# Attention and FFN layer on one core: the PSUM banks of scores and maximum products divided 3 and 3 instead of 4 and 2

## What is computed

```python
B, S, D, H, R = (2, 2048, 256, 16, 64)        # head width 16
qkv = layernorm(x) @ W_qkv + b_qkv            # split into q, k, v; q / 4
dist = clip(key - query, -64, 64) + 64
score = einsum('bhqd,bhkd->bhqk', q, k) + einsum('bhqd,qkd->bhqk', q, rel_emb_k[dist])
attn = softmax(score, axis=-1)
ctx = einsum('bhqk,bhkd->bhqd', attn, v) + einsum('bhqk,qkd->bhqd', attn, rel_emb_v[dist])
x = x + ctx @ W_out + b_out
x = x + ffn_fp4(layernorm(x))
```

## Time and profile before

| what | value |
|---|---|
| median of 3 runs | 2591.05 us (2590.91 to 2592.51) |
| the profiled execution | 2594.04 us, its span 2592.3 us |
| PE busy | 2382.4 us, 92% |
| DVE busy | 1930.2 us, 74% |
| ACT busy | 1361.9 us, 53% |
| POOL busy | 606.9 us, 23% |
| DMA, mean over the span | 81 GB/s |
| PE busy in the 40 slices | 7879999999999999999999999999999993899997 |
| granted clock in the 40 slices, tenths | 9959999999999999999999999999999996999998 |

### The profile page before, as it was taken

How to read it: one execution, slowest core, us unless ns; L and a number is a source line. 1 busy time by engine, 2 the same in 40 slices (tenths; PEclk the granted TensorE clock), 3 DMA queues, 4 the chain that set the end, 5 groups by cost and what they waited for, 6 DMA issues and landing times. The chain is left out here.

```text
span 2592.3 us, 47776 instructions
## 1 busy us (share of the span) xinstructions
PE 2382.4 (92%) x19372; PEld 1179.2 (45%) x19372; DVE 1930.2 (74%) x3509; ACT 1361.9 (53%) x1572; POOL 606.9 (23%) x361
## 2 busy tenths in 40 slices
PE   7879999999999999999999999999999993899997
PEld 3424444444444444444444444444444442566665
DVE  6587777777777777777777777777777726899997
ACT  3405555565555555555555555555555561334442
POOL 5402222222222222222222222222222220011111
PEclk9959999999999999999999999999999996999998
DMA  5723323332333333323332332333222221111110
GB/s 159 184 75 86 85 77 85 88 85 76 85 84 96 93 89 101 99 78 85 85 85 82 93 85 77 85 88 85 76 77 77 71 70 54 43 40 49 49 40 27
DMA packets 275656, 210.35 MB, mean 81 GB/s; under 512 B 17058, under 2 KB 266628, under 8 KB 275332
## 3 DMA queue, kind: packets, MB, share of 16 engines
q1 hardware_dynamic: 274308, 203.37, 28.5%
q0 software_dynamic: 1152, 4.19, 0.6%
HBM read 113.35 MB, written 93.34 MB: 80 GB/s over the span
## 5 line engine op out<-in xcount | busy, mean ns | idle before, releaser
L1047 DVE TENSOR_REDUCE amax<-psA 128x1 f32<-128x512 f32 x2048 | 1327.7, 686 | 494.3 <-PE psA L756 485.9
L1017 ACT ACTIVATE probs<-psS 128x1024 f32<-128x1024 f32 x896 | 885.0, 1023 | 483.5 <-PE psS L867 483.0
L756 PE MATMUL psA<-keys,queries 96*128 96x512 bf16 x2048 | 789.0, 392 | 43.8 <-DVE amax L1047 43.6
L867 PE MATMUL psS<-queries,keys 102*128 102x512 bf16 (+7 forms) x2176 | 632.5, 343 | 44.7 <-ACT rel_scores L996 36.8
L780 PE MATMUL psC<-probs,vals 128*32 128x512 f32 (+7 forms) x4352 | 475.0, 524 | 0.6 <-ACT probs L1017 0.6
L756 PEld LDWEIGHTS psA<-keys,queries 96*128 96x128 bf16 x2048 | 196.4, 97 | 500.5 <-DVE amax L1047 439.2
L717 POOL TENSOR_TENSOR band_probs<-band_probs,side 128x2048 f32<-128x2048 f32 x64 | 288.6, 4533 | 559.5 <-PE psC L880 559.5
L867 PEld LDWEIGHTS psS<-queries,keys 102*128 102x128 bf16 (+1 forms) x2176 | 203.4, 99 | 282.0 <-ACT rel_scores L996 98.1
L1012 ACT ACTIVATE band_probs<-psS 128x1024 f32<-128x1024 f32 x128 | 131.1, 1024 | 224.1 <-PE psS L854 224.1
L996 ACT COPY rel_scores<-psS 128x1024 f32<-128x1024 f32 x128 | 129.3, 1012 | 106.9 <-PE psS L769 106.9
L780 PEld LDWEIGHTS psC<-probs,vals 128*32 128x32 f32 (+1 forms) x4352 | 89.1, 102 | 174.0 <-issue 166.5
(11 more groups left out here) (162 smaller groups left out, 2054.2 us busy)
## 6 DMA issues: line engine op xcount, KB each, us to landing
rel_skew<-rel_scores SPq DMA_DIRECT2D x32, 2048.0 KB, 7.5
rel_near<-rel_skew SPq DMA_DIRECT2D x64, 1024.0 KB, 8.1
keys<-k_ring SPq DMA_DIRECT2D x48, 256.0 KB, 5.7
queries<-q_parts SPq DMA_DIRECT2D x192, 64.0 KB, 2.4
ctx_d<-rden SPq DMA_DIRECT2D x32, 256.0 KB, 2.3
ctx_in<-ctx_d SPq DMA_DIRECT2D x32, 256.0 KB, 2.7
q_parts<-parts SPq DMA_DIRECT2D x16, 384.0 KB, 2.9
k_ring<-parts SPq DMA_DIRECT2D x12, 384.0 KB, 3.1
```

The source lines that it names most:

```text
L756: t.matmul(psA[:, n % 2, :], qs[0:NR, qb, h, u * P:(u + 1) * P], keys[0:NR, par, h, c0:c0 + NQ], start=True, stop=True).then_inc(max_ready, 1)
L867: ins = t.matmul(bank[:, o:o + k], keys[0:nr, par, h, c0:c0 + P], qs[0:nr, qb, h, q0:q0 + k], start=True, stop=True, skip_group_check=True)
L1017: ins = a.activation(probs[:, n % 4], src, ACT.Exp)
L1047: v.reduce_max(amax[:, pair, k:k + 1], psA[:, n % 2, :], AX.X).then_inc(max_taken, 1)
```

## The change

`psS` becomes a ring of three banks, each one half of a unit: half number j (numbered on through the whole attention, R units counted as two halves) lies in bank j modulo 3 and waits for half j - 3. The semaphores `unit_ready` and `unit_done` count halves instead of units, so TensorE signals after each half and ScalarE empties each half in an instruction of its own, 512 elements wide; there are twice as many of these. `psA` becomes a ring of three banks, and product n waits for `take` of product n - 3. No arithmetic is changed. SyncE stores each of the three shift rows once its own part is cut: the first after GpSimd's first cast, the second after its second, the third after the last subtract.

```diff
+SBANKS, ABANKS = 3, 3
-        psS = ctx.enter_context(nc.psum_tensor("psS", [P, 4, NQ], F32))
-        psA = ctx.enter_context(nc.psum_tensor("psA", [P, 2, NQ], F32))
+        psS = ctx.enter_context(nc.psum_tensor("psS", [P, SBANKS, NQ], F32))
+        psA = ctx.enter_context(nc.psum_tensor("psA", [P, ABANKS, NQ], F32))
...
-            def store_shift(qb):
-                for r in range(3):
+            def store_shift(m, qb):
+
+                for r, (cut, count) in enumerate(((m_pool, 3 * m + 1), (m_pool, 3 * m + 3), (shift_ready, m + 1))):
+                    wait_alone(sp, passed, cut, count)
                     sp.dma_start(qs[NR + r:NRH:3, qb], shift[:, r, :]).then_inc(shift_in[qb], 16)
...
-                t.matmul(psA[:, n % 2, :], qs[0:NR, qb, h, u * P:(u + 1) * P], keys[0:NR, par, h, c0:c0 + NQ],
+                t.matmul(psA[:, (first + n) % ABANKS, :], qs[0:NR, qb, h, u * P:(u + 1) * P], keys[0:NR, par, h, c0:c0 + NQ],
...
             def rel_products(m, qb, k, at):
 
-                pe.wait_ge(unit_done, at + 1)
                 for i in range(4):
-                    bank = psS[:, 2 * (k % 2) + i // 2, :]
+                    if i % 2 == 0:
+                        pe.wait_ge(unit_done, 2 * at + i // 2 + 1)
+                    bank = psS[:, (2 * at + i // 2) % SBANKS, :]
...
-                def unit_free(n):
-
-                    pe.wait_ge(unit_done, base + place(n, ends) + 1)
+                def half_free(n, half):
+
+                    pe.wait_ge(unit_done, 2 * (base + place(n, ends)) + half + 1)
...
                 def far_half(n, half):
-                    if half == 0:
-                        unit_free(n)
+                    half_free(n, half)
                     step = n // 2
                     h = 2 * (n % 2) + half
-                    bank = psS[:, 2 * (place(n, ends) % 2) + half, :]
+                    bank = psS[:, (2 * (base + place(n, ends)) + half) % SBANKS, :]
...
-                    if half == 1:
-                        ins.then_inc(unit_ready, 1)
+                    ins.then_inc(unit_ready, 1)
...
-                act.wait_ge(unit_ready, at + 1)
-                a.copy(rel[:, 4 * k:4 * k + 4, :].rearrange("p (b x) r -> p b (x r)", b=2),
-                       psS[:, 2 * (k % 2):2 * (k % 2) + 2, :]).then_inc(unit_done, 1)
+                for half in range(2):
+                    act.wait_ge(unit_ready, 2 * at + half + 1)
+                    x = 4 * k + 2 * half
+                    a.copy(rel[:, x:x + 2, :].rearrange("p x r -> p (x r)"), psS[:, (2 * at + half) % SBANKS, :]).then_inc(unit_done, 1)
...
-                v.reduce_max(amax[:, pair, k:k + 1], psA[:, n % 2, :], AX.X).then_inc(max_taken, 1)
+                v.reduce_max(amax[:, pair, k:k + 1], psA[:, (first + n) % ABANKS, :], AX.X).then_inc(max_taken, 1)
```

More of the change, by code:

```diff
@@ L672, in ctx_rows @@
                 return dr.ctx[bass.ds(b * KT + qb * CH, CH), :, gg, :].rearrange("i p t -> p i t")
-            turn_diagonals(0, RUNITS + 2)
-            wait_alone(sp, passed, shift_ready, 1)
-            store_shift(0)
+            turn_diagonals(0, RUNITS)
+            store_shift(0, 0)
             iteration(0, 0)
@@ L764, in rel_products @@
             def rel_products(m, qb, k, at):
-                pe.wait_ge(unit_done, at + 1)
                 for i in range(4):
-                    bank = psS[:, 2 * (k % 2) + i // 2, :]
+                    if i % 2 == 0:
+                        pe.wait_ge(unit_done, 2 * at + i // 2 + 1)
+                    bank = psS[:, (2 * at + i // 2) % SBANKS, :]
                     ins = t.matmul(bank[:, (i % 2) * DREL:(i % 2 + 1) * DREL], qs[0:NR, qb, k, i * P:(i + 1) * P], c.rel_rows[:],
                                    start=True, stop=True, skip_group_check=True)
-                ins.then_inc(unit_ready, 1)
+                    if i % 2:
+                        ins.then_inc(unit_ready, 1)
             def far_values(g, qb, step, ends=False):
-                pe.wait_ge(unit_done, first_of(g * QB + qb) + place(2 * step + 1, ends) + 1 + 2)
+                pe.wait_ge(unit_done, 2 * (first_of(g * QB + qb) + place(2 * step + 1, ends) + 1) + SBANKS)
                 for o, tile, q0, k in pieces(qb, step):
@@ L868, in far_half @@
                                        qs[0:nr, qb, h, q0:q0 + k], start=True, stop=True, skip_group_check=True)
-                    if half == 1:
-                        ins.then_inc(unit_ready, 1)
+                    ins.then_inc(unit_ready, 1)
                 def band_values():
-                    pe.wait_ge(unit_done, base + 2 * BAND_STEPS + 2)
+                    pe.wait_ge(unit_done, 2 * (base + 2 * BAND_STEPS) + SBANKS)
                     pe.wait_ge(ctx_copied, it + 1)
@@ L1007, in iteration @@
                         copy_context(it - 1)
[L1008 to L1018, removed]
+                    for half in range(2):
+                        act.wait_ge(unit_ready, 2 * (base + place(n, ends)) + half + 1)
+                        src = psS[:, (2 * (base + place(n, ends)) + half) % SBANKS, :]
+                        if n < 2 * BAND_STEPS:
+                            e, c2 = divmod(n, 2)
+                            ins = a.activation(band[:, e, 2 * c2 + half].rearrange("p u q -> p (u q)"), src, ACT.Exp)
+                        else:
+                            if n % 2 == 0 and half == 0:
+                                act.wait_ge(pv_done, it * VALUE_STEPS + n // 2 - BAND_STEPS + 1)
+                            ins = a.activation(probs[:, n % 4, half], src, ACT.Exp)
+                        ins.then_inc(unit_done, 1)
                     if n % 2 == 1 and RSTEP <= n // 2 < RSTEP + RUNITS and not ends:
@@ L1023, in iteration @@
                     copy_context(it)
-            act.sem_inc(unit_done, 2)
+            act.sem_inc(unit_done, SBANKS)
             act.sem_inc(ctx_copied, 1)
@@ L1113, in iteration @@
                     normalise(it)
-            dve.sem_inc(max_taken, 2)
+            dve.sem_inc(max_taken, ABANKS)
             dve.sem_inc(misc_taken, 1)
```

13 lines of the change are left out of this document (6 added, 7 removed).

## The result

The changed kernel takes **2487.0 us** (median; 2485.6 to 2488.5), where the kernel before took 2591.8 beside it: ratio **0.959**, 95% interval 0.958 to 0.961. Run once more beside other kernels it gave 2486.9 (ratio 0.960, 0.958 to 0.961). The forecast was 2491.

What follows compares the result with a forecast made beforehand. TensorE's queue was taken as the bound. 3.1 us a round, 96 over 31 rounds, plus 6.9 and 1.2 in the prologue minus 4 in the last round gave 100 us: 2491 us forecast (72%), range 2462 to 2535.

Steps and rivals of the forecast that it cites:

- Prices: ScalarE on halves: exponential 0.59 us, copy 0.58, starts 0.49 apart; a bank of scores turns round in 1.06.
- Three banks of scores: Steps with R: values product 2.63 or 2.40 us behind R, gaining 0.50 or 0.14; together 1.3 us a round.
- S2 and S3: Third and fourth halves of scores behind R, expected still 0.26 and 0.05 us late.
- the margin: Steps without R: a bank turns in 1.06 us, its next use is 1.10 later; 0.04 to spare, no loss.
- Three banks of products: Steps 0 and 1 gain 1.15 us a round; prologue takes run at 0.60 instead of 0.695, 6.9 us once.
- The stores: Shift rows: last store issued 1.2 us earlier, worth 0.1 a round and 1.2 once in the prologue.
- The last round: No maximum products fill the fourth half's wait; steps last 2.35 instead of 2.08 us, 4 us lost.
- the six small waits: Six other maximum products a round start 0.07 to 0.15 us late; all 0.6 a round goes.
- The fixed cost shows: Rival, 16%: short ScalarE instructions do not overlap, halves 0.58 to 0.59 apart, 25 us less gained: 2516 us.
- VectorE is the bound anyway: Rival, 5%: maximum products wait as long as now; 2.5 us a round and the prologue's 6.9 missing: 2575 us.
- The small ring strangles TensorE: Rival, 4%, slower: a half's exponential takes 0.75 us at 0.75 spacing, a bank's turn becomes 1.22: 2629 us.
- the break-even: Scores ring: from about 0.72 us for a half's exponential and spacing, the small ring decides against the change.

Runs made afterwards that it cites:

- the last experiments: Changed kernel with maximum products moved into remaining waits behind R (2473.1, then 2454.1 us) and in step 3 (2451.2); then values product ahead of fourth half, last round (2448.7).
- two copies ahead: Changed kernel with two single-column ScalarE copies ahead of each half's exponential, after its wait: 2575.7 us, ratio 0.994 to the kernel before.

## Why the prediction was right

**What bounds.** Right: TensorE's queue, with waits seen only as distances. With most of the waits removed its records fill 61.5 of 62 us.

**Prices.** The exponential of a half is recorded for 0.61 and 0.60 (taken 0.59), the copy for 0.59 (0.58). Four exponentials take 2.08, so they start 0.49 apart, as taken: the overlap of long ones holds for short ones. With 0.61 it is 0.12 and not 0.10, so two errors of 0.02 cancel in the 0.49. The estimate of 0.57 us from the Trainium skill, "VectorE: DVE Perf Modes", section on the TRN2 errata, lies under the recorded 0.59 to 0.61. The prediction read the Trainium skill's advice on tile size in that section as speaking against the change; but it asks for tiles of at least 512 elements, which the halves have, and it is about reads from SBUF, where these are from PSUM. The case that the prediction priced beside it, no overlap, would have been worth 25 us that did not come: 2516 against 2487.

**Three banks of scores.** R to V 2.65 and 2.44, forecast 2.63 and 2.40. That S2 and S3 would still wait was right, and the last experiments put work there. Where no M stands ahead of V less was gained than forecast, 0.09 a step instead of 0.14. The kernel before, then the changed one:

```profile
1018.99 0.61 PE L769 MATMUL psS<-rel_rows,queries 96*128 96x256 bf16 x4
...
1021.51 1.07 PE L780 MATMUL psC<-probs,vals 128*32 128x512 f32 x8
```

```profile
1024.15 0.61 PE L772 MATMUL psS<-rel_rows,queries 96*128 96x256 bf16 x4
...
1026.58 1.06 PE L784 MATMUL psC<-probs,vals 128*32 128x512 f32 x8
```

The bank's turn of 1.06 is read as 1.08 with two banks, and as 1.08 in the last round (below), where S3 waits for it. So the margin was 0.02 rather than 0.04, and it behaves as said: a copy that adds 0.10 moves S3 from 1.10 to 1.17.

**Three banks of products.** The prediction speaks of thirteen Ms in steps 0 and 1; `ORDER` has fourteen there, and the sum, which uses the last ten, is not touched. Steps 0 and 1 in the changed kernel, TensorE, then VectorE (beside the earlier trace rows):

```profile
1000.63 0.81 PE L758 MATMUL psA<-keys,queries 96*128 96x512 bf16 x3
...
1005.08 0.70 PE L758 MATMUL psA<-keys,queries 96*128 96x512 bf16 x2
```

```profile
1001.05 6.07 DVE L1049 TENSOR_REDUCE amax<-psA 128x1 f32<-128x512 f32 x10 [0.19 <-PE psA L758]
```

Ten products from 1000.63 to 1005.08 + 0.31 = 1005.39: 4.76, forecast 1059.86 - 1055.10 = 4.76. VectorE takes ten in one run, 0.60 apart, and is the limit there. In the prologue 64 takes last

```profile
130.04 38.34 DVE L1049 TENSOR_REDUCE amax<-psA 128x1 f32<-128x512 f32 x64
```

0.60 each instead of 0.695. The prologue gained 9.2 where 6.9 + 1.2 stood in the sum. All 73 takes gave the 6.9 and the stores 1.3. The other 1 us was left out of the sum: 0.5 lies in the R units ahead of the takes, and 0.4 behind the takes, since with a third bank T is issued one take earlier.

**The stores.** The mechanism was right. The last store is issued 0.22 behind GpSimd's last part, where it was 1.43 before; the 1.2 came, though not the 0.1 that the prediction named as the sign. The first wait for the stores went from 4.96 to 3.64 us, 1.3. Taken alone, the edit is worth 8.7 us in the changed kernel and not 4 or so. That is no error of the sum: the way from T to the first matmul that needs the shift rows went from 5.96 to 5.77, nearly all of it 0.10 for the stores and 0.07 for the M of step 14, and the sum has both. Without the new stores both are lost.

**The last round.** 3.3 lost, 4 forecast (3.6 up to the last reciprocal); steps of 2.39 instead of 2.08:

```profile
2006.81 0.82 PE L868 MATMUL psS<-queries,keys 99*128 99x512 bf16 x3
2007.89 0.39 PE L868 MATMUL psS<-queries,keys 99*128 99x512 bf16 x1 [0.26 <-ACT probs L1019]
...
2013.98 0.82 PE L868 MATMUL psS<-queries,keys 99*128 99x512 bf16 x3
```

**The sum.** 31 rounds gained 99.8, forecast 96. Of the 3.8 between them, 1.6 is rounding: the terms of a round add up to 3.15, not 3.1. From V to V, a round in the middle of attention gained just those 3.15, but not by the terms as forecast. The R steps gave 1.12 instead of 1.3. In their place stand 0.11 in step 3, which was left out (V is 2.38 behind the first half after B instead of 2.50), and 0.67 instead of 0.6 for the six small waits. That these errors, worth some 5 us each way, cancel is luck. The other 2.2 us lie in rounds unlike the rest, 1.5 of them in the first; why is open. With 1.1 more in the prologue and 0.7 less lost in the last round, the sum comes out 4 to 6 us short of the measured gain: 104.8 by the medians, 106.1 between the two traces.

**The rivals.** *The fixed cost shows*: fell with the spacing of 0.49. *VectorE is the bound anyway*: VectorE is busy 48 of 62 us, and 395 us of its idle time end with a product from TensorE. *The small ring strangles TensorE*: not with three banks and this exponential, but it is real. It was made to happen twice, by a bank less (2697) and by slower halves; with two copies ahead a turn is 1.26, halves are 0.66 apart, and the kernel is within 0.6% of the one before. I had put the break-even at 0.72 for both the exponential and the spacing (a turn of 1.19). With a longer turn but a closer spacing than that, the two copies come near it; so the place was about right, but no kernel here has both numbers as priced.

## What to carry to other kernels

When one queue feeds two consumers through two rings of banks, lay out one period of it by hand with four numbers: the distance of free starts, the way from a start to its reader, the reader's recorded time, and the way back. A ring has enough banks when its turn is shorter than the distance to the place where the bank is used next; count that distance in the real order, and for both rings, since a bank given to one gains nothing where the other is the later. Then look at what the shortened period no longer covers, and place independent work into the waits that stay.

## What the runs showed of the hardware

- On ScalarE the second of two instructions in a row starts 0.09 to 0.12 us before the recorded end of the first: at 1024 elements 0.92 apart at a recorded 1.02, at 512 0.49 at 0.61, and behind a copy of one column 0.10 at 0.19. This copy so costs a tenth of a microsecond in a chain, not the 0.2 that its record shows.
- VectorE's takes of 512 from PSUM run 0.60 apart at a recorded 0.69, over runs of ten and of 64.
- The FFN, the same code in all kernels, took between 441 and 449 us in the profiled executions. The granted clock of its first 147 us does not order them (0.75: 447.6 us, 0.79: 441.6, 0.81: 446.6). The spread is as much as the last experiments gain, so small steps are better read from the stretch that they change.
